# Mixing matrices by four DMA copies, a product in four parts, and stacked biases and gates

## The reference

```python
# layer 0: mix, then a mixture of experts with a shared expert
h = einsum('bct,bcd->bdt', x, weights[condition])        # 16 matrices of 32 x 32
logits = xt @ router_w + router_b                        # xt: 1024 tokens x 512
scores = softmax(logits) + router_bias                   # 16 experts in 4 groups
...                                                      # best 2 groups, best 2 experts in them
for w1, b1, w2, b2, w3, b3, ge in experts:               # 16 experts, inner width 128
    y = y + ge[:, None] * ((silu(xt @ w1 + b1) * (xt @ w2 + b2)) @ w3 + b3)
z = silu(xt @ sw1 + sb1) * (xt @ sw2 + sb2) @ sw3 + sb3  # shared expert, inner width 256
x = x + y + z
# layer 1: long convolution in time with a kernel made from log_dt, C, A, then a dense layer
kernel = 2 * einsum('hn,hnl->hl', Cs, exp(dtA * arange(512))).real
y = irfft(rfft(u * mask) * rfft(kernel))[..., :512] + u * mask * D;  y = y * mask
h = relu(y @ up_w) ** 2 @ down_w
scale = sum of the two largest of (y @ gate_w)           # 8 columns
x = x + layernorm(h + ((y @ fc1_w) @ expert_w * scale) @ fc2_w) * ln_gamma + ln_beta
```

## Time and profile before

| | |
|---|---|
| median of 3 runs | 343.67 us (340.64 to 344.4) |
| the profiled execution | 343.47 us, span 341.6 us |
| TensorE busy | 324.8 us (95%) |
| VectorE busy | 187.4 us (55%) |
| ScalarE busy | 115.3 us (34%) |
| GpSimd busy | 109.8 us (32%) |

### The profile page before, as it was taken

One profiled execution on the slowest core, in us unless ns is written; L12 is line 12 of the kernel. 1 busy time (PEld: TensorE's weight loads), 2 busy tenths in 40 slices (PEclk: granted clock), 3 DMA queues, 4 the chain that ended last, 5 costly groups with the idle time before them and its releaser, 6 DMA issues.

```text
span 341.6 us, 5497 instructions
## 1 busy us (share of the span) xinstructions
PE 324.8 (95%) x1945; PEld 245.8 (72%) x1945; DVE 187.4 (55%) x375; ACT 115.3 (34%) x199; POOL 109.8 (32%) x131
## 2 busy tenths in 40 slices
PE   8998899999999599999998899899999999999994
PEld 2566788988887288888686444468888787888872
DVE  3747896888365122365469469537322446442366
ACT  1571312323722123363006833832231424222120
POOL 8243004356577546663400000699200000000000
PEclk9999999999999879999999999999999999999999
DMA  6999920796686629999969986000000000100002
GB/s 194 327 405 405 384 70 13 221 316 205 188 269 219 199 69 328 317 318 378 406 236 412 388 279 216 2 1 0 2 0 0 3 0 31 63 31 0 2 21 101
DMA packets 32830, 59.93 MB, mean 175 GB/s; under 512 B 7213, under 2 KB 8081, under 8 KB 32804
## 3 DMA queue, kind: packets, MB, share of 16 engines
q1 hardware_dynamic: 25764, 48.95, 41.6%
q0 software_dynamic: 4992, 8.42, 7.2%
q10 hardware_dynamic: 2048, 2.21, 1.8%
HBM read 55.02 MB, written 12.40 MB: 197 GB/s over the span
## 4 chain that ended last, share of the span: by engine, by line
PE 80%; DVE 10%; issue 5%; POOL 2%; ACT 2%; DMA 1%; ACTq 0%; DVEq 0%; POOLq 0%
PE bank L1606 15%; PE bank L435 13%; PE bank L437 12%; PE bank L436 12%; PE bank L1574 7%; PE bank L1679 5%; PE bank L1568 4%; PE bank L1434 2%; DVE acc L1259 2%; PE bank L1688 1%; PE bank L1384 1%; PE bank L1466 1%; PE bank L1390 1%; PE bank L1509 1%; DVE osum L1307 1%
## 5 line engine op out<-in xcount | busy, mean ns | idle before, releaser
L1606 PE MATMUL bank<-xt,ew 128*128 128x128 f32 x496 | 62.4, 280 | 0.0
L1606 PEld LDWEIGHTS bank<-xt,ew 128*128 128x128 f32 x496 | 59.6, 196 | 0.8 <-issue 0.7
L639 POOL DMA_INDIRECT xg<-xrow,tokx x31 | 33.3, 1073 | 38.9 <-DVE tokx L1077 25.2
L646 POOL DMA_INDIRECT ytok<-yout,dstx x31 | 31.9, 1029 | 33.3 <-DVE yout L1189 20.3
L1348 DVE TENSOR_TENSOR sq<-rel 128x512 f32<-128x512 f32 x16 | 13.3, 834 | 37.0 <-ACT rel L888 37.0
L1574 PE MATMUL bank<-ew,bhid 128*128 128x512 f32 x62 | 31.7, 595 | 0.0
L792 ACT ACTIVATE xt<-bank 128x512 f32<-128x512 f32 x31 | 18.4, 598 | 31.9 <-PE bank L1568 24.6
L1568 PEld LDWEIGHTS bank<-ident,xg 128*128 128x128 f32 x124 | 15.1, 141 | 16.1 <-issue 14.0
L435 PE MATMUL bank<-ah,uph 128*128 128x512 f32 x64 | 25.2, 394 | 0.9 <-issue 0.9
L435 PE MATMUL bank<-dnh,sqh 128*128 128x512 f32 x64 | 25.2, 393 | 0.4
L436 PE MATMUL bank<-dnl,sqh 128*128 128x512 f32 x64 | 24.9, 390 | 0.0
(11 more groups left out here) (316 smaller groups left out, 619.5 us busy)
## 6 DMA issues: line engine op xcount, KB each, us to landing
ew<-in_L_ffn_ew SPq DMA_DIRECT2D x51, 256.0 KB
ew<-in_L_ffn_ew SPq DMA_DIRECT2D x21, 512.0 KB, 11.9
toep<-kpad SPq DMA_DIRECT2D x4, 1536.0 KB, 17.6
acc<-in_x SPq DMA_DIRECT2D x4, 512.0 KB, 7.2
xrow<-xstage ACTq DMA_DIRECT2D x4, 512.0 KB, 7.7
yg_lo<-ytok SPq DMA_DIRECT2D x4, 512.0 KB, 4.9
yg_hi<-ytok SPq DMA_DIRECT2D x4, 512.0 KB, 8.1
upraw<-in_L_ffn_up_w SPq DMA_DIRECT2D x1, 2048.0 KB, 14.3
```

The lines of the kernel that those rows point to most:

```text
L639: pool.indirect_dma_start(xg[:, n % XGS, :], None, xrow, bass.IndirectOffsetOnAxis(ap=tokx[:, n:n + 1].bitcast(U32), axis=0), bounds_check ...
L646: pool.indirect_dma_start(ytok, bass.IndirectOffsetOnAxis(ap=dstx[:, n:n + 1].bitcast(U32), axis=0), yout[:, n % YOS, :], None, bounds_che ...
L1606: mm = pe.matmul(bank[2 + n % 2][:, w * P:(w + 1) * P], ew[:, ring(n), col + k * P:col + (k + 1) * P], xt[:, n % 2, k, :], start=(k == 0), ...
```

## The change

`wraw` is now loaded four times, once for each group of 32 partitions, and the copies onto the diagonal read it there. A stack of the 18 turned gates in `gth` (rows 0 and 64 high, row 32 low) meets a stack of the biases in `b3h` (rows 0 and 32 high, row 64 low), so one matmul gives the three products. Two small matrices add high and low logits as they are turned back. The small products of the time kernel stand in blocks 14 to 17, eight in each. The `leni` loads go from SyncE to GpSimd, where one of two zeroing products goes. The rank products stand one step later, `split_lo(0)` one tile earlier.

```diff
-    LIST_STEP = 4
+    LIST_STEP = 8
+    B3_ROWS = (0, 32, 64)
+    KSTEP = 14
-    wraw = at(r, "wraw", [C, NCOND, C])
+    wraw = at(r, "wraw", [P, NCOND, C])
-    gtl = at(r, "gtl", [P, N], F32R)
-    b3l = at(r3, "b3l", [P, T], F32R)
+    sum16 = at(small, "sum16", [2 * E, E])
+    sum8 = at(small, "sum8", [2 * NE1, NE1])
...
 # ScalarE: the loads and the picking
-        act.dma_start(wraw[:, :, :], cond_w.rearrange("k c d -> c k d")).then_inc(wraw_in, 16)
+        for b in range(BT):
+            act.dma_start(wraw[b * C:(b + 1) * C, :, :], cond_w.rearrange("k c d -> c k d")).then_inc(wraw_in, 16)
-        act.wait_ge(wall_done, 2)
+        act.wait_ge(wraw_in, 16 * BT)
-                act.activation(diagonal(i, b), matrix(7, b, conds[b]), ACT.Copy).then_inc(wbd2_ok, 1)
+                act.activation(diagonal(i, b), matrix(b, conds[b]), ACT.Copy).then_inc(wbd2_ok, 1)
...
 # TensorE: the spreading products go
-        pe.wait_ge(wraw_in, 16)
-        for w in (6, 7):
-            for b in range(BT):
-                mm = pe.matmul(bank[w][b * C:(b + 1) * C, :], ident[0:C, 0:C],
-                               wraw[:, :, :].rearrange("c k d -> c (k d)"), start=True, stop=True)
-            mm.then_inc(wall_done, 1)
...
 # VectorE
+        for dst, n in ((sum16, E), (sum8, NE1)):
+            tt(dst[:, :], ident[0:2 * n, 0:n], ident[0:2 * n, n:2 * n], ALU.add).then_inc(sums_ok, 1)
-        dve.wait_ge(wall_done, 1)
+        dve.wait_ge(wraw_in, 16 * BT)
-                dve.tensor_copy(diagonal(i, b), matrix(6, b, conds[b])).then_inc(wbd_ok, 1)
+                dve.tensor_copy(diagonal(i, b), matrix(b, conds[b])).then_inc(wbd_ok, 1)
+            if i == 4:
+                split_lo(0)
             if i == 5:
-                split_lo(0)
-        link(tt(sc[:, :, :], lgv[:, :, 1, :], rows(rb[:, 0, :], E), ALU.add))
-        link(tt(sc[:, :, :], lgv[:, :, 0, :], sc[:, :, :], ALU.add))
+        link(tt(sc[:, :, :], bank[5][:, 0:NT * E].rearrange("p (i e) -> p i e", e=E), rows(rb[:, 0, :], E), ALU.add))
...
 # gates, biases
-            act.activation(gth[0:G, j * HALF:(j + 1) * HALF], bank[4 + j][0:G, :], ACT.Copy).then_inc(gt_ok, 1)
+            for row in (B3_ROWS[0], B3_ROWS[2]):
+                act.activation(gth[row:row + G, j * HALF:(j + 1) * HALF], bank[4 + j][0:G, :], ACT.Copy).then_inc(gt_ok, 1)
-            dve.wait_ge(gt_ok, 2 * j + 1)
-            tt(gtl[0:G, j * HALF:(j + 1) * HALF], bank[4 + j][0:G, :], f(gth[0:G, j * HALF:(j + 1) * HALF]), ALU.subtract)\
-                .then_inc(gt_ok, 1)
+            dve.wait_ge(gt_ok, 3 * j + 2)
+            row = B3_ROWS[1]
+            tt(gth[row:row + G, j * HALF:(j + 1) * HALF], bank[4 + j][0:G, :], f(gth[0:G, j * HALF:(j + 1) * HALF]),
+               ALU.subtract).then_inc(gt_ok, 1)
-        tt(b3l[:, :], b3p[:, :], f(b3h[:, :]), ALU.subtract).then_inc(b3z_ok, 1)
+        low = slice(B3_ROWS[2], P)
+        tt(b3h[low, :], b3p[low, :], f(b3h[low, :]), ALU.subtract).then_inc(b3z_ok, 1)
-            split3(pe, bank[B3BANK[i % len(B3BANK)]][:, :], lambda _: (gth[:, s], gtl[:, s]),
-                   lambda _: (b3h[:, :], b3l[:, :]), 1).then_inc(b3_done, 1)
+            pe.matmul(bank[B3BANK[i % len(B3BANK)]][:, :], gth[:, s], b3h[:, :], start=True, stop=True).then_inc(b3_done, 1)
...
 # rank products
-            split3(pe, bank[CBANK[1]][:, :], weights, tokens, 1, stop=False)
+            split3(pe, bank[CBANK[1]][:, :], weights, tokens, 2, stop=False)
             rank_products()
...
 # the time kernel: TensorE, ScalarE (n of kout), VectorE (n of its last add), SyncE (n of the stores)
-            if n == 15:
+            if KSTEP <= n < KSTEP + HT // KQ:
...
-                for m in range(HT // KQ):
+                m = n - KSTEP
-            if n == 16:
-                act.wait_ge(k_done, 1)
+            if n == 18:
+                act.wait_ge(k_done, HT // KQ)
-            elif n == 17:
+            elif n == 19:
-            if n == 18:
+            if n == 20:
                 sp.wait_ge(s4v_ok, SKIP)
```

More of the change, by code:

```diff
@@ L230, in adaln_ffn_program @@
     hotb = at(r, "hotb", [P, K * NT, 2, NSLOT], F32R)
-    gtl = at(r, "gtl", [P, N], F32R)
-    zrow = f(gtl[C:2 * C, 0:P])
     r = [raw_at + KC * INT1 * 4]
@@ L258, in adaln_ffn_program @@
     gth = at(small, "gth", [P, N], F32R)
+    zrow = f(gth[3 * C:4 * C, 0:P])
     gam = at(r, "gam", [P, T])
     bet = at(r, "bet", [P, T])
-    r3 = list(small)
     b3p = at(small, "b3p", [P, T])
-    b3l = at(r3, "b3l", [P, T], F32R)
-    b3m = b3p[0:G, :]
     b3h = at(small, "b3h", [P, T], F32R)
@@ L445, in picked_matrices, with matrix @@
         return conds
-    def matrix(w, b, k):
-        return bank[w][b * C:(b + 1) * C, :].rearrange("p (k d) -> p k d", d=C)[:, bass.ds(k, 1), :]
+    def matrix(b, k):
+        return wraw[b * C:(b + 1) * C, bass.ds(k, 1), :]
     def diagonal(i, b):
@@ L480, in _ @@
         sp.wait_ge(drowz_ok, 1)
-        sp.dma_start(b3m[0:1, :], sb3.rearrange("(o n) -> o n", o=1)).then_inc(l1_in, 16)
-        sp.dma_start(b3m[SH:G, :], eb3).then_inc(l1_in, 16)
-        for j in range(BT):
-            sp.dma_start(leni[j * B:(j + 1) * B, :], length.rearrange("(b o) -> b o", o=1)).then_inc(len_in, 16)
+        for row in B3_ROWS:
+            sp.dma_start(b3p[row:row + 1, :], sb3.rearrange("(o n) -> o n", o=1)).then_inc(l1_in, 16)
+            sp.dma_start(b3p[row + SH:row + G, :], eb3).then_inc(l1_in, 16)
         sp.dma_start(drow[LI - 1:P:P // KQ, :], d_param.rearrange("(o n) -> o n", o=KQ)).then_inc(l1_in, 16)
@@ L597, in _ @@
                            0.0, None, ALU.mult).then_inc(gates_ok, 1)
-        pool.tensor_scalar(gtl[:, :].rearrange("p (i n) -> p i n", n=P), prow[:, :].unsqueeze(1).broadcast_to([P, NT, P]),
-                           0.0, None, ALU.mult).then_inc(gates_ok, 1)
+        for j in range(BT):
+            pool.dma_start(leni[j * B:(j + 1) * B, :], length.rearrange("(b o) -> b o", o=1)).then_inc(len_in, 16)
         def split_hi(n):
@@ L934, in _ @@
                 prow[:, 0:E].unsqueeze(2).broadcast_to([P, E, E]), ALU.is_lt))
+        dve.wait_ge(wraw_in, 16 * BT)
+        for i, conds in dve_conds:
+            for b in range(BT):
+                dve.tensor_copy(diagonal(i, b), matrix(b, conds[b])).then_inc(wbd_ok, 1)
         dve.wait_ge(rw_ok, 1)
@@ L1450, in logits_back @@
             pe.wait_ge(lgt_ok, p + 1)
+            pe.wait_ge(sums_ok, 1)
             for i in range(2 * p, 2 * p + 2):
-                mm = pe.transpose(bank[5][:, i * 2 * E:(i + 1) * 2 * E], ltr[:, i // TH, i % TH * P:(i % TH + 1) * P],
-                                  ident[0:2 * E, 0:2 * E])
+                mm = pe.matmul(bank[5][:, i * E:(i + 1) * E], ltr[:, i // TH, i % TH * P:(i % TH + 1) * P], sum16[:, :],
+                               start=True, stop=True)
             return mm
@@ L1621, in _ @@
                 mm.then_inc(bd_done, 1)
-            if n == 15:
-                pe.wait_ge(bd_ok, 1)
-                pe.wait_ge(lhs_ok, 2)
-                for m in range(HT // KQ):
-                    for lhs, rhs in ((lre_k, rre_k), (lim_k, rim_k)):
-                        for q in range(KQ):
-                            t = q * HT // KQ + m
-                            mm = pe.matmul(bank[4][q * P // KQ:q * P // KQ + LI, m * 2 * LJ:(m + 1) * 2 * LJ], lhs[:, t, :],
-                                           rhs[:, t, :, :].rearrange("p a j -> p (a j)"), start=(lhs is lre_k),
-                                           stop=(lhs is lim_k))
+            if KSTEP <= n < KSTEP + HT // KQ:
+                if n == KSTEP:
+                    pe.wait_ge(bd_ok, 1)
+                    pe.wait_ge(lhs_ok, 2)
+                m = n - KSTEP
+                for lhs, rhs in ((lre_k, rre_k), (lim_k, rim_k)):
+                    for q in range(KQ):
+                        t = q * HT // KQ + m
+                        mm = pe.matmul(bank[4][q * P // KQ:q * P // KQ + LI, m * 2 * LJ:(m + 1) * 2 * LJ], lhs[:, t, :],
+                                       rhs[:, t, :, :].rearrange("p a j -> p (a j)"), start=(lhs is lre_k),
+                                       stop=(lhs is lim_k))
                 mm.then_inc(k_done, 1)
@@ L1712, in gates_back @@
             pe.wait_ge(lgt_ok, NT // 2 + 2)
+            pe.wait_ge(sums_ok, 2)
             for i in range(NT):
-                mm = pe.transpose(bank[2][:, i * 2 * NE1:(i + 1) * 2 * NE1],
-                                  ltg[:, i // TH, i % TH * P:(i % TH + 1) * P], ident[0:2 * NE1, 0:2 * NE1])
+                mm = pe.matmul(bank[2][:, i * NE1:(i + 1) * NE1], ltg[:, i // TH, i % TH * P:(i % TH + 1) * P], sum8[:, :],
+                               start=True, stop=True)
             mm.then_inc(lg_done, 1)
```

29 lines of the change are left out of this document (12 added, 17 removed).

## The result

The changed kernel takes 352.38 us (median of 4 runs, 350.65 to 353.08) against 342.67 for the kernel before (4 runs on the same chip): ratio 1.0289, interval 1.0236 to 1.0341. It is slower by 9.7 us; forecast were 340.4 us and a range of 335 to 348.5. Its profiled execution took 353.08 us, span 351.4, which is 9.8 over the span of before (341.6). One thing has to be known for all that follows: executions with the same or nearly the same code up to the first shared product reach it early (25.4 to 26.0 us) or late (28.7 to 29.2 us), and the profiled execution of before is a late one (28.98).

A forecast was written before the change was run, and what follows sets the result against it. TensorE was taken to bound the kernel, with 80% of the chain of waits. From 343.47 us, +4.1 (start), -2.1 (routing to b3), -6.4 (time kernel) and +1.3 (kpad) gave 340.4 us, range 335 to 348.5.

The forecast's parts named there:

- Start, +4.1: Kernel start: picking waits for all four wraw copies, so the first mixing product starts at 12.9 us, 4.1 us later.
- The landing that I took at 12.0: Kernel start: the fourth wraw copy lands at 12.0 us, held up by queues taking turns beside x.
- the 16.4 of the ratio of packets: Rival 3, kernel start: by the measured packet ratio the copies land at 16.4 us, total 344.8; chance 0.08.
- Routing, gates, lists and b3, -2.1: Stretch up to the one-hot transpose: fewer b3 matmuls, VectorE's adds set the pace, -1.8; with swl earlier, -2.1 us.
- The wait of one us that I expected of TensorE: End of the b3 stretch: TensorE waits about one microsecond before the one-hot transpose at 63.4 us.
- The time kernel in four parts, -6.4: Expert loop behind block 15: four parts of 16 records remove the gaps and the slow clock, -6.4 us.
- Rival 1: Block 15 stall comes from late semaphores and busy GpSimd and DMA, and returns: 346.8 us; chance 0.27.
- `kpad`, +1.3: Blocks 23 to 26: ScalarE waits for the later kpad stores, delaying block 26 by 1.3 us (0 to +2.5).
- The blocks behind it have their operands in time: Expert loop after block 26: no further delay from the kpad wait beyond its +1.3 us.
- Sums of logits, 0 to 0.2: Second layer's logits: the one-matmul sums lie beside running products and cost nothing, 0.2 us at most.
- the two terms taken as small: The kpad wait at blocks 23 to 26, +1.3 us, and the second layer's sums of logits, 0 to 0.2.

The follow-up runs named there:

- b_copies: Kernel before with only the four copies of wraw and no spreading products; 1.0141 of the kernel before.
- b_b3: Kernel before with only the b3 term made one product; 0.9958 of the kernel before.
- b_coef: Kernel before with one edit: the fifteen small steps for the S4 coefficients moved from GpSimd to VectorE; 0.9879 of the kernel before.
- a_readers: Changed kernel with the readers of kpad_in (sw3h, hidh, sw3l, hidl) moved two blocks later; 1.0194 of the kernel before.

## Why the prediction was wrong

Point by point, in its own order:

- **Start, +4.1: in size not refuted.** Against the profiled execution of before it was +2.9 at the first mixing product and +2.3 at the first shared product, but that execution has the late start; `b_copies` alone costs 4.8 us (3.7 to 6.0) by its runs. The landing that I took at 12.0 was at 10.62. The Trainium skill, DMA: Bandwidth & Descriptors, section "Queues, rings and completion order", has each DMA engine take turns between rows of queues, packet by packet. I had made that turns piece by piece, which gave 11 to 13. The landing is near to it and far from the 16.4 of the ratio of packets, but the turns were not of that kind. From 3.8 to 5.0 us in the changed kernel ScalarE's queue (q10) moved almost three packets to one of SyncE's (q1), as the profile counts them:

```profile
q1 hardware_dynamic: 186, 0.35, 76.9%
q10 hardware_dynamic: 523, 0.06, 35.1%
```

So the near hit of the landing is luck in part, and the share that small pieces get isn't settled. The picking was no quicker from SBUF (6.46 us for 28) than from PSUM (6.08).
- **Routing, gates, lists and b3, -2.1: right, -1.7.** The stretch started 2.3 late and ended 0.6 late; eight adds ran in 4.92 us without the gap of the earlier trace rows, and `b_b3` alone shortens it by 1.8. The wait of one us that I expected of TensorE ahead of the one-hot's transpose isn't there.
- **The time kernel in four parts, -6.4: this step failed, with 0 won.** It took the place of the gaps for their cause. The gaps lay among the 64 records because those stood there when GpSimd's row of transfers reached its end; in the changed kernel they lie in other instructions, and in `b_coef` 64 records in a row take 1.02 us. What makes the stall is GpSimd's row of eleven transfers: paced, they leave two gaps of 0.28 and 0.43 us of it. Rival 1 (late semaphores, a busy GpSimd) had it right, and the earlier trace rows with its "remote" was the evidence; I gave it 0.27. In place of -6.4 the stretch from block 1 to 25 got 1.0 longer.
- **`kpad`, +1.3: mis-sized, +5.4.** The stores were issued at 147.43, and their weight load at 146.09, not at 144.32, as the loop was 1.6 late; they landed at 154.1, not at 151.7. TensorE's own loss at block 26 was 1.9. Missing was what hangs on a block that is late near the loop's end: a gather, the scatters, the `yg` loads and the combining sums, 3.5 more. "The blocks behind it have their operands in time" was wrong. `a_readers` brought 3.7 of the 5.4 back. (The rows for these blocks are the earlier trace rows; the prediction's first paragraph points at the earlier trace rows.)
- **Sums of logits, 0 to 0.2: mis-sized, +2.8.** Eight of these products make sixteen records where eight transposes made eight, each 0.118 us against 0.075, on a TensorE that is busy throughout there; I had counted the work as hidden. That is 1.3 of the 2.8; the rest is the half clock, which two of five traces with these products don't have.

By the stretches of the two traces: 2.3 - 1.7 + 1.0 + 5.4 + 2.8 = 9.8, which must come out, as they cover the span; that the parts alone make 10.6 by their own runs is the independent check, within their intervals. With the stall's return alone I had 346.8; the two terms taken as small make up most of the rest.

## What to carry to other kernels

A stretch of gaps in which several engines start late with no named releaser isn't the fault of the instructions that happen to stand there: look at what every other engine is doing, GpSimd first, and test by moving that. Compare traces from the point where their code begins to differ: two executions of the same code were 3.3 us apart before block 0, more than most of these edits are worth. A later store is charged to whoever waits for it, and near the end of a loop a wait travels on through gathers, scatters and reloads, so that its price is more than TensorE's own idle time. Turning a transpose and a small add into a matrix product is only free where TensorE has idle time.
